# One decoder layer on one core: the first pair's normalisation and query moved ahead of a block boundary, scatters without their last wait, 32 constant products instead of 34

## The reference

```python
x = x + attn(layernorm(x))         # token diffusion (16 heads), then channel diffusion (8 heads)
x = x + xattn(layernorm(x), ctx)   # 16 heads of depth 8; 56 queries on 1500 keys per batch
x = x + ffn(layernorm(x))          # 8 experts of width 512, two chosen per token

def _channel_diffusion(x, Wqk, Wv, Wo, tau):
    dot = jnp.einsum('bhcn,bhdn->bhcd', qk, qk)
    logits = (2.0 * dot - q2[..., :, None] - q2[..., None, :]) / math.sqrt(n) * tau
    attn = jax.nn.softmax(logits, axis=-1)
    return out @ Wo                  # out = attn applied to v
def _L0_xattn_ref(query, value, ...):
    q = _split_heads(query @ wq.T + bq, B)
    attn = jax.nn.softmax(jnp.einsum('bhqd,bhkd->bhqk', q, k) / scale, axis=-1)
def _moe_forward(...):
    top_v, top_i = jax.lax.top_k(x_flat @ gate_w.T, K)      # K = 2
```

## Time and profile before

| what | value |
|---|---|
| time, median of 3 runs | 569.3 us (569.18 to 570.83) |
| time of the profiled execution | 569.5 us |
| its span, first to last instruction | 567.3 us |
| mean granted TensorE clock | 0.96 of full |
| busy in the span | PE 90%, DVE 70%, ACT 57%, POOL 50% |
| block boundary | about 90 to 91.5 us |
| cross attention proper | about 118 to 472 us |
| scatters and constants | about 471 to 495.6 us |

### The profile page before, as it was taken

One profiled execution on the slowest core, in us unless ns is written; L12 is line 12 of the kernel. 1 busy time (PEld: TensorE's weight loads), 2 busy tenths in 40 slices (PEclk: granted clock), 3 DMA queues, 4 the chain that ended last, 5 costly groups with the idle time before them and its releaser, 6 DMA issues.

```text
span 567.3 us, 17072 instructions
## 1 busy us (share of the span) xinstructions
PE 513.2 (90%) x6485; PEld 429.9 (76%) x6485; DVE 396.5 (70%) x809; ACT 322.4 (57%) x500; POOL 286.2 (50%) x212
## 2 busy tenths in 40 slices
PE   2699997789999999999999999999999894899991
PEld 1466664467888888888888888888888783899991
DVE  4867576876777877877778788788787682434552
ACT  2466574427566667576576676575765661136760
POOL 4485425654773663664745736737642106523331
PEclk9989998869999999999999999999999988699997
DMA  6009004488755747638547557376375237411103
GB/s 249 1 2 324 23 2 105 76 167 192 165 145 131 163 109 163 143 93 191 117 107 167 132 135 163 105 166 144 87 151 113 61 107 275 153 50 52 50 24 120
DMA packets 30976, 69.77 MB, mean 123 GB/s; under 512 B 15148, under 2 KB 19372, under 8 KB 30852
## 3 DMA queue, kind: packets, MB, share of 16 engines
q1 hardware_dynamic: 29752, 66.77, 47.7%
q0 software_dynamic: 1184, 2.44, 1.2%
HBM read 27.88 MB, written 7.82 MB: 63 GB/s over the span
## 4 chain that ended last, share of the span: by engine, by line
PE 68%; SPq 4%; DVE 4%; ACT 2%; issue 2%; DMA 2%; POOL 1%; ACTq 0%; POOLq 0%
PE PS L1811 14%; PE PS L1835 14%; PE PS L1851 13%; PE PS L1998 7%; PE PS L245 5%; PE PS L2012 3%; DVE chunk_max L1482 2%; PE PS L1864 2%; PE PS L2017 2%; SPq L1156 2%; PE PS L1865 2%; PE PS L1866 2%; ACT k_full L259 1%; SPq L1149 1%; PE PS L1872 1%
## 5 line engine op out<-in xcount | busy, mean ns | idle before, releaser
L1482 DVE TENSOR_REDUCE chunk_max<-PS 128x1 f32<-128x500 f32 x336 | 212.8, 674 | 57.1 <-PE PS L1811 57.0
L1363 ACT ACTIVATE P<-PS 125x896 f32<-125x896 f32 x192 | 171.4, 914 | 127.1 <-PE PS L1835 124.8
L1811 PE MATMUL PS<-k_hi,q_block_hi 128*128 128x500 f32 x336 | 130.6, 439 | 5.4 <-DVE chunk_max L1482 2.9
L268 POOL TENSOR_TENSOR k_lo<-k_full,k_hi 128x500 fp32r<-128x500 f32 x48 | 60.5, 1261 | 130.8 <-ACT k_full L259 130.8
L1835 PE MATMUL PS<-q_stack,k_stack 97*125 97x224 f32 x768 | 121.1, 281 | 2.0 <-ACT P L1363 1.2
L1835 PEld LDWEIGHTS PS<-q_stack,k_stack 97*125 97x125 f32 x768 | 109.0, 190 | 15.9 <-ACT P L1363 6.0
L1851 PE MATMUL PS<-P,values 125*32 125x112 f32 x3072 | 85.0, 263 | 0.8 <-issue 0.7
L1851 PEld LDWEIGHTS PS<-P,values 125*32 125x32 f32 x3072 | 73.2, 111 | 15.7 <-issue 10.3
L1811 PEld LDWEIGHTS PS<-k_hi,q_block_hi 128*128 128x128 f32 x336 | 62.0, 195 | 25.0 <-DVE chunk_max L1482 11.5
L245 PE MATMUL PS<-mats,ctxT 128*125 128x128 f32 x384 | 50.0, 274 | 0.0
L1266 POOL TENSOR_TENSOR ctx_lo<-ctxT,ctx_hi 128x1500 fp32r<-128x1500 f32 x14 | 47.7, 3406 | 1.1
(11 more groups left out here) (205 smaller groups left out, 711.0 us busy)
## 6 DMA issues: line engine op xcount, KB each, us to landing
k_stack<-k_hi SPq DMA_DIRECT2D x128, 187.5 KB, 4.5
ctxT<-ctx_in SPq DMA_DIRECT2D x16, 750.0 KB, 4.3
k_stack<-k_lo SPq DMA_DIRECT2D x64, 187.5 KB, 4.5
slots<-slots_in SPq DMA_DIRECT2D x1, 4615.0 KB
experts<-wgu_in SPq DMA_DIRECT2D x8, 512.0 KB, 5.8
experts<-wd_in SPq DMA_DIRECT2D x8, 256.0 KB, 7.1
q_stack<-neg_rows SPq DMA_DIRECT2D x112, 0.5 KB, 1.7
tokens<-slots SPq DMA_DIRECT2D x21, 65.0 KB, 1.9
```

What stands on the lines that cost most here:

```text
L268: nc.gpsimd.tensor_tensor(k_lo[:, j, k], k_full[:, k], k_hi[:, j, k].bitcast(F32), ALU.subtract).then_inc(k_lo_ready, 1)
L1363: nc.scalar.activation(P[:, t % RING, :].rearrange("p (a n) -> p a n", a=2), PS[0:KR, 2 * (t % 2):2 * (t % 2) + 2, 0:HALF], ACT.Exp).then_ ...
L1482: nc.vector.tensor_reduce(out=chunk_max[:, n // KC, n % KC:n % KC + 1], in_=PS[:, max_bank(b, n), 0:KW], axis=AX.X, op=ALU.max).then_inc(m ...
L1811: nc.tensor.matmul(PS[:, max_bank(b, n), 0:KW], q_block_hi[:, j, 128 * t:128 * t + 128], k_hi[:, j, KW * c:KW * c + KW], start=True, stop= ...
```

## The change

Three edits. First, the statistics, the `rstd`, the normalisation, the transpose and the query projection of pair 0 move from the start of the second block to the end of the first; they use other PSUM places (bank 4) and `Y` instead of `Y2`. Second, POOL's wait for the last scores ahead of the first scatter goes. Third, 32 products of constants instead of 34.

```diff
@@ POOL, first block
                     split_keys(pool, 0, 0, 0)
+                    layernorm_power(pool, 4, slice(0, 1))
@@ ACT, first block
                     copy_mixed(1)
+                    copy_y2(act, 0, T[:, 0:2 * PITCH], PS[:, 4, 2 * PITCH:4 * PITCH])
@@ DVE, first block
                         read_values(dve, 0, 0, c, VALUE_BANKS[c])
+                    dve.wait_ge(x1_ready, 1)
+                    step.mark(take_stats(X, range(1)))
+                    step.wait()
+                    join_stats(range(1))
+                    take_stats(X, range(1, 4))
+                    dve.wait_ge(rstd_ready, 5)
+                    nc.vector.tensor_scalar(Y[:, 0, :], X[:, 0, :], moments[:, 0, 0:1], rstd[:, 0:1], ALU.subtract, ALU.mult
+                                            ).then_inc(y2_ready, 1)
                     add_mixed(1)
@@ PE, first block
                     project_mixed(1)
+                    pe.wait_ge(y2_ready, 1)
+                    nc.tensor.transpose(PS[:, 4, 2 * PITCH:4 * PITCH], Y[:, 0, :], C["ident"]).then_inc(y2_turned, 1)
+                    pe.wait_ge(y2_copied, 1)
+                    nc.tensor.matmul(FIRST_QUERY, MAT["wq"], T[:, 0:2 * PITCH], start=True, stop=True).then_inc(q_projected, 1)
@@ second block: the same instructions go on POOL, ACT (copy_y2), DVE and PE
                     first_key(0)
                     first_key(1)
-                    pe.wait_ge(y2_ready, 1)
-                    nc.tensor.transpose(PS[:, 1, 0:2 * PITCH], Y2[:, 0, :], C["ident"]).then_inc(y2_turned, 1)
-                    pe.wait_ge(y2_copied, 1)
-                    nc.tensor.matmul(PS[:, 0, 0:2 * PITCH], MAT["wq"], T[:, 0:2 * PITCH], start=True, stop=True
-                                     ).then_inc(q_projected, 1)
                     pe.wait_ge(k_ready, KC + 1)
@@ POOL, scatters
                     pool.wait_ge(slots_cleared, 32)
-                    pool.wait_ge(s_done, KT * B)
                     pool.wait_ge(slots_ready, 1)
@@ PE, constants
-                    for i in range(34):
+                    for i in range(32):
                         nc.tensor.matmul(PS[:, 6, 0:128], C["ident"], C["ones"], start=True, stop=True)
```

More of the change, by code:

```diff
@@ L142, in build @@
         slots_cleared = sem("slots_cleared")
+        y2_ready = sem("y2_ready")
+        y2_turned = sem("y2_turned")
+        y2_copied = sem("y2_copied")
+        q_projected = sem("q_projected")
         steps_of = {}
@@ L228, in build, with copy_y2 @@
         SPARE = PS[:, 6, :]
+        FIRST_QUERY = PS[:, 4, 0:2 * PITCH]
+        def copy_y2(act, c, dst, src):
+            act.wait_ge(y2_turned, c + 1)
+            nc.scalar.copy(dst, src).then_inc(y2_copied, 1)
         def load_ctx(sp, b, j):
@@ L1090, in build @@
             assert FREE[1] == 7
-            y2_ready = sem("y2_ready")
             shift_negated = sem("shift_negated")
             y2_rest = sem("y2_rest")
-            y2_turned = sem("y2_turned")
-            y2_copied = sem("y2_copied")
-            q_projected = sem("q_projected")
             q_scaled = sem("q_scaled")
@@ L1226, in _ @@
                 def _(pool):
-                    layernorm_power(pool, 4, slice(0, 1))
                     pool.wait_ge(rstd_ready, 5)
@@ L1327, in _ @@
                 def _(act):
-                    def copy_y2(c, dst, src):
-                        act.wait_ge(y2_turned, c + 1)
-                        nc.scalar.copy(dst, src).then_inc(y2_copied, 1)
                     nc.scalar.copy(wk_hi[:, :], MAT["wk"]).then_inc(wk_split, 1)
                     read_keys(act, 1, 1, 0, 0, FIRST_KEY_BANKS[0])
-                    copy_y2(0, T[:, 0:2 * PITCH], PS[:, 1, 0:2 * PITCH])
                     for c in range(1, KC):
@@ L1343, in _ @@
                     for c, part in enumerate(REST):
-                        copy_y2(c + 1, T[:, part], PS[:, 6:8, :].rearrange("p a n -> p (a n)")[:, part])
+                        copy_y2(act, c + 1, T[:, part], PS[:, 6:8, :].rearrange("p a n -> p (a n)")[:, part])
                     for c, part in enumerate(REST):
@@ L1449, in _ @@
                     step = steps_of["dve"].again(dve)
[L1450 to L1456, removed]
                     step.mark(take_stats(X, range(4, PAIRS)))
@@ L1463, in _ @@
                     dve.wait_ge(q_projected, 1)
-                    step.mark(nc.vector.tensor_scalar(q_all[:, first], PS[:, 0, first], COL["bq"], DH ** -0.5,
+                    step.mark(nc.vector.tensor_scalar(q_all[:, first], FIRST_QUERY, COL["bq"], DH ** -0.5,
                                                       ALU.add, ALU.mult))
```

## The result

The changed kernel took 567.99 us (median of 20 runs, 565.72 to 570.10) beside 570.87 us of the kernel before on the same chip (20 runs, 567.78 to 574.38): a ratio of 0.9946 (95% interval 0.9932 to 0.9961), some 3.1 us. Forecast were 3.0 us. The time named, 566.3 us, was counted from the 569.3 us of three runs; with 20 runs the kernel before has 570.87, so 567.99 lies near the upper end of the stated range (568.2). The profiled execution of the changed kernel took 565.77 us, its span 563.6 (before: 567.3).

What follows compares the result with a forecast made beforehand. PE holds 68% of the chain and sets attention's pace, so only its ends could win: 1.6 us front plus 1.4 back, 3.0 off the profiled 569.5, median 0.2 lower: 566.3 us, range 565.3 to 568.2.

Steps and rivals of the forecast that it cites:

- The front edit ahead of the boundary: End of first block: moved work fits DVE's 3.0 us hole, DVE stays last at the barrier; cost 0, up to 0.2 us.
- They stay.: Start of second block: PE's first two key products stay at 91.71 to 95.22 us, at 1.2 GHz.
- Now it starts at 95.2 and ends at 96.2: Second block: the third key product, before at 96.00 us, follows the first two directly; maxima start 1.8 us earlier.
- The rival that was given 8%: Boundary: PE's clock stays up, two key products take half of 3.51 us, 0.3 us more gets through: 566.0 us; 8%.
- ACT gains less than DVE ... I take 0.5: Second block: ACT's normalisation of pairs 1 to 7 comes only 0.5 us earlier, DVE's maxima 1.8.
- The lower bound: Front gain shrinks to 0.5 us if all 2.83 us from ACT's normalisation to chunk 9 followed ACT.
- The cap: Front: SP is busy to 108.39 us, then issues four shifts to 110.9, so the gain is at most 1.9 us.
- the sum: Whole kernel: 1.6 us at the front plus 1.4 us at the scatters, 3.0 us won.
- The shift reaches 141.7 and PE carries it through attention: Batch 1's last shift, at 141.7 us before, comes earlier by the front's 1.6 us, kept through attention.
- The front as a term: Block boundary to attention: 1.6 us won, bounds 0.9 to 1.9.
- the new wait: Back end: after six earlier scatters POOL's last-pair `rstd` waits for its moments, starting at 477.15 us, 1.4 earlier.
- Slower: Experts: PE arrives at 1.2 GHz, and three stretches at half rate turn -3.0 into +2.2 us: 571.5 us; 6%.

Runs made afterwards that it cites:

- e8: Kernel before, plus five products of constants on PE between the first block's last mixed key projection and the barrier: 572.25 us, one execution (kernel before 573.05).
- e5: Changed kernel, with SP loading the context of batch 2 at the head of the second block instead of behind the shifts: 575.83 us, ratio 1.0031.
- e2: Kernel before, without POOL's wait for the last scores ahead of the scatters, still 34 products: 570.08 us, ratio 0.9979.
- e4: Changed kernel, with 34 products of constants instead of 32: 568.94 us, ratio 0.9983.
- e6: Kernel before, with the context of batch 2 issued first in the second block: 573.32 us, one execution (kernel before: median 574.19).
- e10: Changed kernel run again with nothing altered, for a second profile: 575.99 us, ratio 1.0030 against the kernel before.
- e1: Changed kernel, with POOL's old wait back and 34 products, so the front edit alone: 569.27 us, ratio 0.9988.
- e9: Kernel before, with POOL's memset of the row of ones moved behind its two means of the first pair: 575.41 us, one execution.

## Why the prediction was right, and where it was not

**The front edit ahead of the boundary: right.** The normalisation was forecast at 88.0 us with 0.34, it ran at 87.83 with 0.34. PE's last product before the barrier was forecast to end at 90.6, it ended at 90.59. DVE was last, as forecast. That the barrier opens 0.4 us sooner was not foreseen: it opens 0.30 us behind DVE's end, before 0.66. Why isn't known.

**The two key products: "They stay."** This step failed, and with it "Now it starts at 95.2 and ends at 96.2" for the third key product, which ran at 93.78. The forecast had taken the 3.51 us with the clock that belonged to the old idle time; they are 1.91. The clock stays up in all eight profiled kernels with the front edit and falls in five of the six with the old front; e8, the sixth, shows that PE's work before the barrier is the cause. The rival that was given 8% happened. The Trainium skill, in "TensorE: Matmul & The Clock Gate", "What's actually happening", has the low rate as the default, which activity releases; the trace agrees (granted 1.00 behind an idle time of 0.71 us, 0.50 behind 2.17). The first maximum came at 95.15 us, not 96.6.

**"ACT gains less than DVE ... I take 0.5": wrong, by the same step.** ACT's normalisation of pairs 1 to 7 started at 96.11 us, before at 98.24, so 2.1 us sooner. The lower bound never came into play: the maxima went through without a wait, and the second negated rows came at 108.48 us, not 110.9.

**The cap: right, and what saved the sum.** "SP is busy to 108.39 us whatever the others do": it was busy to 108.05, then sent seven shifts in 4.37 us. Of 4.0 us that the negated rows had won, SP passed on 2.1, the barrier's 0.4 included in both.

**"The shift reaches 141.7 and PE carries it through attention": half right.** Behind SP's cap stood a chain that the prediction didn't follow: third context, POOL's split, PE. It gave PE a wait of 2.32 us and then 3.4 us at the low clock, which at half rate is up to 1.7 us (an estimate from the windows), and the copy of batch 1 comes at 76.55 us in the mean of the six executions that have the new front and SP's old order (76.15 to 77.29), against 77.29 in the mean of four with the old front: of what SP had passed on, 0.7 us are left. From there to the copy of batch 14 it is carried to 0.1 us (364.39 against 365.19). e5 shows that SP's queue stands behind this: without the context's wait the next shifts are late, and the low clock comes there. The last pair gives 0.86 more. Its stretch at 1.2 GHz (3.4 us before) stands in all six kernels with the old front and is missing in all eight with the new; that this is the 0.86 us fits, and why it is missing was not tested.

**The front as a term.** Over all, the last scores come at 376.73 us in the mean of six (376.23 to 377.39), with the old front at 378.40 in the mean of four: 1.7 us, and with the barrier 2.0. Forecast were 1.6. That it is so near is luck. The forecast carried 1.6 us from the maxima through attention; 0.7 came that way, some 0.9 from the last pair's clock and 0.4 from the barrier. And the early fall of the clock at the eight products took back 0.3 to 0.9, a term that the forecast put at nothing.

**The second edit: right.** 1.32 us in e2, 1.33 in the changed kernel and 1.35 in e4 for 1.4, and the new wait is the one named: the last pair's `rstd` behind its moments. It holds only where these moments come less than 8.6 us behind the last scores, by when the old order has its six scatters done (1.0 + 7.6 us).

**The third edit: near nothing, as costed, by another sum.** With the scatters earlier and 34 products PE still waited 0.84 us (e2) and 0.63 (e4) for the tile, where the forecast had the products end 0.15 us behind it: it had priced a record at 0.156 us, and e4's 68 took 9.83 us, 0.145 each. On chips B and C it may be most of 0.8 us, which is argued above.

**The rivals.** "Slower" was given 6%, by PE at 1.2 GHz at the experts. The changed kernel was slower on chips B and C, and the largest term there is another mechanism, ACT's wait, for which nothing stood in the trace of before. What it waits for stays open: the loads of weights and the fetch of instructions were named as causes, and no run tested either. That this wait belongs to a chip, and not to an hour, is also only argued, since each chip was used at one time only.

## What to carry to other kernels

A duration read from a trace carries the clock of its place: when an edit fills or opens an idle time ahead of a matmul, price it at both levels. When a stage in front of a queue gets faster, follow the queue's next entries as well as the one that was late: here the third context alone was worth more (2.9 us in e6) than the maxima that had been moved (1.7), and with both the start was no better than with the maxima alone (e5). An engine that comes sooner to a late transfer is idle for longer, and can pay for it in clock. Early context with the new scatters and the old front was not run, and is what to try next.

## What the runs showed of the hardware that was not expected

- The same program had a wait of 0.71 us in its first profile and of 7.0 us on chips B and C, within 0.05 us in every profile, and on those chips the kernels that differ from it far ahead of that place had 3.3.
- On chips B and C PE also stands still among products of constants that wait for nothing: 0.66, 0.45 and 0.35 us in e8, 0.44 in e10, none in e4.
- A stretch at 1.2 GHz moves when an idle time is taken away (e5, from 34 to 48 us behind the opening) and isn't always saved.
- Eight products in the same place took 1.16, 1.42, 1.58 or 2.08 us, by when the granted clock fell from 1.00 to 0.50 (the kernel before, the changed one, e1, e4).
- One GpSimd memset of a row in a single partition (1.34 us) made a DVE normalisation four times as long (1.45 us, 0.35 without it in e9), and left DVE's statistics alone (four in 0.87 us beside it in the changed kernel, 0.86 without it in e9).
